# Late keys zeroed by GpSimd, a running maximum for 256 queries, and TensorE ordered by array mode, in a top-k attention and expert layer

## What is computed

```python
h = layernorm(x) * (1 + ca) + sa
q, k, v = (keep_largest(proj(h, w)) for w in (wq, wk, wv))   # one feature of 16 kept per head
scores = einsum('bhqd,bhkd->bhqk', q, k) / 4
scores = where(key later than query, -inf, scores)
scores = keep the 64 largest of each row, -inf elsewhere       # ties go to the earlier key
x = x + ga * (softmax(scores) @ v) @ wo.T
h = layernorm(x) * (1 + cb) + sb
x = x + gb * ffn(h)      # 8 experts, each takes the 512 tokens that want it most
```

## Time and profile before

| what | value |
|---|---|
| median of 3 runs (lowest, highest) | 1067.7 us (1066.64, 1073.47) |
| span of the profiled execution | 1065.8 us |
| attention, first to last score matmul | 65 to 720 us of the span |
| groups without other sequences' work | 32.8 us each |
| tile groups | 42.1 to 44.0 us |
| groups g = 0 that start and finish a sequence | 45.9 us |

### The profile page before, as it was taken

One profiled execution on the slowest core, in us unless ns is written; L12 is line 12 of the kernel. 1 busy time (PEld: TensorE's weight loads), 2 busy tenths in 40 slices (PEclk: granted clock), 3 DMA queues, 4 the chain that ended last, 5 costly groups with the idle time before them and its releaser, 6 DMA issues. The chain is left out here.

```text
span 1065.8 us, 17246 instructions
## 1 busy us (share of the span) xinstructions
PE 914.5 (86%) x6504; PEld 497.0 (47%) x6504; DVE 662.4 (62%) x1469; ACT 480.1 (45%) x631; POOL 268.7 (25%) x403
## 2 busy tenths in 40 slices
PE   6778999898999988999998999997204999999996
PEld 5533343444444443544445445335102666666664
DVE  6758677568587676676874775735487555543441
ACT  2635767664567745466773654661000122221110
POOL 3603222411331312122230220001003433343322
PEclk9869999999999998999998998998555999999999
DMA  4000000000100002100002011101561244442211
GB/s 145 15 1 21 1 21 1 1 1 2 61 21 1 1 2 81 60 1 2 1 1 81 2 41 44 38 1 40 198 221 37 51 114 107 112 115 41 25 20 20
DMA packets 34854, 46.57 MB, mean 44 GB/s; under 512 B 2184, under 2 KB 30928, under 8 KB 34640
## 3 DMA queue, kind: packets, MB, share of 16 engines
q1 hardware_dynamic: 28624, 36.89, 10.4%
q0 software_dynamic: 6144, 8.52, 5.0%
HBM read 32.69 MB, written 12.72 MB: 43 GB/s over the span
## 5 line engine op out<-in xcount | busy, mean ns | idle before, releaser
L947 ACT ACTIVATE p_buf<-ps 128x1024 f32<-128x1024 f32 x288 | 279.4, 1023 | 181.3 <-PE ps L424 95.6
L424 PE MATMUL ps<-qx,kd 32*128 32x512 f32 (+3 forms) x1280 | 147.0, 536 | 29.8 <-DVE p_buf L1281 26.1
L457 PE MATMUL ps<-p_buf,vv 128*17 128x512 f32 (+3 forms) x1664 | 156.1, 477 | 0.0
L2108 ACT ACTIVATE h_t<-ps,b_t 128x512 f32<-128x512 f32 x64 | 44.0, 688 | 236.7 <-PE ps L2048 236.7
L1281 DVE SCALAR_TENSOR_TENSOR p_buf<-ps,p_buf 128x1024 f32<-128x1024 f32 x64 | 76.7, 1220 | 78.0 <-ACT p_buf L947 65.0
L2048 PE MATMUL ps<-tok_t,w_sb 128*128 128x512 f32 x256 | 113.5, 602 | 0.0
L2058 PE MATMUL ps<-w_sb,h_t 128*128 128x256 f32 x512 | 112.5, 380 | 0.8 <-ACT h_t L2108 0.8
L779 POOL TENSOR_SCALAR_AFFINE_SELECT p_buf<-p_buf 128x512 f32<-128x512 f32 x64 | 42.0, 669 | 272.5 <-ACT p_buf L947 269.7
L2058 PEld LDWEIGHTS ps<-w_sb,h_t 128*128 128x128 f32 x512 | 96.6, 190 | 15.3 <-ACT h_t L2108 1.6
L424 PEld LDWEIGHTS ps<-qx,kd 32*128 32x128 f32 x1280 | 55.2, 191 | 71.6 <-issue 56.2
L365 PE MATMUL ps<-w_t,h_t 128*128 128x512 f32 (+1 forms) x224 | 78.8, 496 | 0.6 <-ACT w_t L889 0.6
(11 more groups left out here) (297 smaller groups left out, 1391.8 us busy)
## 6 DMA issues: line engine op xcount, KB each, us to landing
w_sb<-in_L_ffn_w_dram SPq DMA_DIRECT2D x16, 1024.0 KB, 8.8
h_table<-xr SPq DMA_DIRECT2D x3, 1056.0 KB, 4.6
x_in<-in_L_attn_x_dram SPq DMA_DIRECT2D x6, 512.0 KB, 3.9
out_dram<-xr SPq DMA_DIRECT2D x3, 1024.0 KB, 5.2
xr<-in_L_attn_x_dram SPq DMA_DIRECT2D x3, 1024.0 KB, 5.8
h_table<-xr SPq DMA_DIRECT2D x2, 528.0 KB, 3.0
xr<-in_L_attn_x_dram SPq DMA_DIRECT2D x2, 512.0 KB, 5.3
p_buf<-in_L_wmod_dram SPq DMA_DIRECT2D x1, 1024.0 KB, 8.6
```

The source lines that it names most:

```text
L424: m = pe.matmul(o, key, qx[r, par, t0:t0 + w], start=True, stop=not early)
L457: m = pe.matmul(ps[32 * h:32 * h + HD + 1, 6, o:o + w], vv[:, (gi // NG) % 2, i, HG * (gi % NG) + h, :], p_of(gi, u)[:, h, lo:lo + w], sta ...
L947: act.activation(p_of(gi, u)[:, 2 * a:2 * a + 2, :], buf(w), ACT.Exp, scale=0.25).then_inc(free_of(w)[0], 1)
L2108: act.activation(h1_t[:, f, :], ps[:, L1_BANKS[f % 3], :], ACT.Relu, bias=b1_t[:, e * FO + f:e * FO + f + 1]).then_inc(s_h1, 1)
```

## The change

1. `late` is gone. GpSimd's `tri` now also runs for units 0 and 1 and zeroes every diagonal block, eight a group where it was four. Values of units 0, 1, 2, 3 and 8 wait for it. In GpSimd's order `tri(gi, 0)` and `tri(gi, 1)` stand just ahead of `tri(gi, 2)`, behind `keep` of the first tile and `first_rstd`.
2. The running maximum and its correction cover 256 queries (`RUN`): `over` runs on 128 columns of unit 0 and 256 of unit 1, and `mx`, `qm`, their scan and the reduction beside it change length. The factor in `over` becomes -0.625.
3. TensorE's order in a block becomes scores and `chosen`'s first matmuls, then whole-array steps, then values. `chosen(gi, 0, 1)` moves behind unit 2's scores, `chosen(gi, 1, 0)` behind unit 5's, `chosen(gi, 1, 1)` behind unit 6's; `project` moves ahead of the values; unit 4's values go behind unit 5's, at the end of block 7; `lost` moves from the end of a group to behind unit 0's scores of the next.
4. VectorE follows: `negatives(gi)` at a group's start, `mask(gi, 1, 0)` ahead of `keys` (and behind the second norm and the layer norm's statistics), `mask(gi, 1, 1)` behind `keys` and behind `one_feature` of the third tile. ScalarE takes `out_bank(gi-1, 1)` after `evict_y`.

```diff
-        DIAG = (2, 3, 8)
+        DIAG = (0, 1, 2, 3, 8)
...
-                        early = t0 < 512
-                        diag = early and t0 == P * i
+                        run = max(min(RUN - t0, w), 0)
...
-                        for h in range(HG * diag):
-                            o = buf(("S", gi, u, h // 2))[:, h % 2, lo:lo + P]
-                            m = pe.matmul(o, identb[:, :], late[:, :], start=False, stop=True)
+                            o = buf(("S", gi, u, h // 2))[:, h % 2, lo:lo + run]
+                            m = pe.matmul(o, over[r, :], qm[r, par, t0:t0 + run], start=False, stop=True)
...
                 def pv(gi, u):
-                    if u in (3, 8):
+                    if u in DIAG:
                         pe.wait_ge(f_tri, tri_of(gi, u))
...
                     scores(gi, 0)
+                    lost(gi)
                     if gi:
                         pv(gi - 1, 7)
...
                     scores(gi, 1)
                     chosen(gi, 0, 0)
+                    if more:
+                        rows("K0", n)
+                    if tiles:
+                        project(b + 1, t0)
                     if gi:
                         pv(gi - 1, 8)
...
+                    scores(gi, 2)
                     chosen(gi, 0, 1)
                     if more:
                         rows("K1", n)
                     pv(gi, 0)
...
                     scores(gi, 5)
+                    chosen(gi, 1, 0)
...
                     scores(gi, 6)
+                    chosen(gi, 1, 1)
                     turn_back(gi, 0)
-                    pv(gi, 4)
...
                     if tiles:
                         keep(b + 1, t0)
+                    tri(gi, 0)
+                    tri(gi, 1)
                     tri(gi, 2)
                     tri(gi, 3)
...
+                    mask(gi, 1, 0)
                     if more:
                         keys(n)
                     if tiles:
                         one_feature(b + 1, t0 + 2)
+                    mask(gi, 1, 1)
                     out_rows_of(gi, 0)
```

## The result

The changed kernel takes 1111.3 us (1107.8 to 1113.5) against 1070.2 for the kernel before beside it: ratio 1.039, interval 1.035 to 1.043. The span of the profiled execution grew from 1065.8 to 1111.4 us, all of it in attention: from unit 1 of the first group to the end of attention it is 736.4 us after 689.0 (unit 1 begins 1.5 us earlier), and the experts' part takes 306 us in both. That is 45.6 us where the medians differ by 41.1: the profiled execution of the kernel before lies 2.5 us under that median, the one after 2.0 above its own.

A forecast was written before the change was run, and what follows sets the result against it. Attention was taken as bound by TensorE's own work and its waits: -30.6 work, -11.5 order, -41 waits that leave, +73 GpSimd wait with clock, +43 VectorE waits, sum +33 us. That gave 1067.7 + 33 = 1101 us, range 1070 to 1124.

The forecast's parts named there:

- Work that leaves: Units 0 to 2 on TensorE: `late` and shorter `over` save 1.91 us a group, 30.6 us in 16 groups.
- Order: TensorE's blocks: six fewer array mode changes a group on average, 0.12 us each, save 11.5 us.
- the rival of dear mode changes: TensorE's mode changes cost 0.29 us instead of 0.12, 38 us less: 1063 us, no change; chance 0.14.
- The new wait for GpSimd: Unit 0's values wait for `tri(gi, 0)` behind `keep` or `first_rstd` in nine groups, adding 60 us.
- Nothing is paid back: Behind the waits at unit 0's values ScalarE and VectorE run dry too, so the waiting is not recovered.
- Clock: TensorE's half-clock stretches, 1.4 us each: 13 us added behind nine GpSimd waits, 11 saved at unit 5's scores.
- the 6 us at `spread_mod`: Half clock behind `spread_mod`'s wait for VectorE in four groups finishing a sequence, 1.4 us each.
- Waits that leave and new ones for VectorE: Waits at unit 5's scores and `lost` leave, 41 us with clock; waits at `zero_rank`, `spread_mod` add 43 net.
- the ring: With second masks' entries behind units 5 and 6, unit 5's scores no longer wait for a mask: 25 us saved.
- GpSimd in time: Rival at unit 0's values: `tri(gi, 0)` done when TensorE arrives, 73 us go: 1028 us; chance 0.07.
- Masks at 1.70 us: Grown-waits rival: GpSimd's masks at 1.70 us in the nine-wait chain, +19 us; chance 0.17 for grown waits together.
- The half clock: Grown-waits rival: half clock twice as long behind the 13 long waits, +18 us; chance 0.17 for grown waits together.

The follow-up runs named there:

- Experiment 2: Kernel before with the work's part alone (`late` gone, eight masks, 256 queries), old orders, `tri(gi, 0)` and `tri(gi, 1)` first on GpSimd: 1043.9 us, ratio 0.977.
- experiment 7: Kernel before with the new order of `lost`, `chosen(gi, 0, 1)`, `rows`, `project` and `out_bank`, second masks' order excluded: 1071.2 us, ratio 1.001.
- experiment 5: Changed kernel with `tri(gi, 0)`, `tri(gi, 1)` and `tri(gi, 2)` moved to the head of GpSimd's group: 1051.7 us, ratio 0.983.
- experiment 3: Kernel before with the order's part of the change alone (points 3 and 4), `late` and `over` as before: 1087.8 us, ratio 1.015.
- Experiment 10: Experiment 2 with `tri(gi, 0)` and `tri(gi, 1)` behind `first_rstd` and `keep`, TensorE's order still old: 1094.2 us, ratio 1.023.
- experiment 12: Changed kernel with matmuls that nobody reads filling the nine waits ahead of unit 0's values: 1093.8 us, ratio 1.022.
- experiment 6: Kernel before with the second masks' new order alone, unit 4's values behind unit 5's with it: 1076.1 us, ratio 1.007.
- experiment 4: Changed kernel with `tri(gi, 0)`, `tri(gi, 1)` first on GpSimd, `chosen(gi, 1, 1)` behind `chosen(gi, 1, 0)`, both second masks ahead of `keys`: 1058.2 us, ratio 0.991.
- experiment 8: Experiment 2 with `tri(gi, 2)` first too, `chosen(gi, 1, 0)` behind unit 5's scores, `chosen(gi, 1, 1)` behind the small steps after: 1058.9 us, ratio 0.989.

## Why the prediction was right

It said 1101 us in 1070 to 1124, slower; 1111.3 came, and the forecast's own mechanism, the wait for GpSimd, made most of it. That the number came so near is partly luck, since errors of both signs cancel. In attention the profiled executions differ by 47.4 us where the sum has 33: the clock took some 10 us more than forecast and waits for ScalarE 16 more, while waits for VectorE took 8 less, and 2 to 3 us more of work left than forecast. By its steps:

- **Work that leaves, 30.6 us.** Experiment 2: 31.6 us of busy time. In the kernel before unit 0 goes from its scores (692.01) to the values behind it (694.18 in the earlier trace rows) in 2.17 us, in the kernel after from its scores to `lost` in 1.20: 0.97 us less, where 0.93 was forecast. One row of the kernel before, two of the kernel after:

```profile
692.01 0.93 PE L424 MATMUL ps<-qx,kd 32*128 32x384 f32 x8
...
483.55 0.93 PE L421 MATMUL ps<-qx,kd 32*128 32x384 f32 x8
...
484.75 0.23 PE L400 MATMUL ps<-upto,lw 128*128 128x128 bf16 x1
```

- **Order, 11.5 us.** Right in size, as far as runs tell: 13.0 us of busy time in experiment 7, 11.2 between experiments 2 and 5, and 4.9 in experiment 3, where the clock took some 8 us back (17 us more at 0.50). The bound of 0.29 us a change is out, and with it the rival of dear mode changes: by it experiment 2 would have lost 52 us of busy time, not 31.6. The Trainium skill (TensorEngine Tiling (Array Packing), Key Properties) has TensorE drain at each change; no run here shows more than the 0.12 us estimated from the earlier trace rows for one.
- **The new wait for GpSimd, 60 us.** 59.9 in nine waits; in a tile group 6.2 to 6.5 (6.4 forecast), in the two g = 0 5.5 (5.6), in the first 10.9 (10.6). The chain from the mask's start took 6.65 us of the 6.9. Experiment 10 gave 44.0 us where 44 was worked out in the same way. A chain of durations through in-order engines can be summed from the old trace.
- **"Nothing is paid back".** Nearly: wait (60) and clock (17.5) are 77 us, and three masks moved take 60 off. From the kernel after to experiment 5 idle time falls by 46 us only: 2.2 us of waiting for GpSimd stay, scores wait 7 us longer for ScalarE, and the waits for VectorE grow by 5.
- **Clock, 13 us behind the nine waits, 11 back at unit 5's scores.** Both missed to the same side. The nine waits cost 17.5 us by experiment 12. And nothing came back: in experiment 6 the wait at unit 5's scores is gone, and TensorE is busy at the granted clock 0.50 for 67 us of attention, after 65. With the 6 us at `spread_mod` the sum has 8 us for the clock; in the kernel after 105 us run at 0.50, 40 more than before, some 18 us lost (estimate by 2.09 against 1.14 us for a unit of scores).
- **Waits that leave and new ones for VectorE, -41 and +43.** The wait at unit 5's scores went, as said, and new ones came at `zero_rank`, `spread_mod` and scores of units 6 and 7. Without the clock the step makes these waits 8 us longer; they did not change: TensorE waits 46.0 us for VectorE in attention before, and 46.0 after. Up to the last score all fourteen kernels have 35 to 44 us of them. So TensorE's order chooses where it waits for VectorE, and hardly how long in all. That VectorE's chain of masks, `keys` and `out_rows_of` is what fixes this sum is argued, not shown; and VectorE doesn't set the pace alone, since experiment 2 took 31.6 us off TensorE's work and these waits stayed at 40 us up to the last score.
- **What the sum lacked: ScalarE.** Scores, transposes and projections wait 17.8 us for it in the kernel after (three lines shown), where scores waited 3.5 before; in all it is 23.6 us in attention after 7.1. The step that failed is the ring: I followed it for VectorE's masks alone. Single `chosen` entries between the units leave the next unit's scores with an entry that was given out later than before, and ScalarE has only just begun to read it. The places bear this out. Of the 10.7 us of scores, 9.4 stand at units 2, 3 and 7, each next in the ring behind a single `chosen`, where the kernel before has 0.3. Experiment 7, which parts only the first two, has the waits at units 2 and 3 and none at 7. Behind the fourth, at unit 6, it is only 0.4 us, so the account isn't complete.

The same two gaps show in experiment 3, expected at -10 and found at +18: ScalarE's waits and the clock, with no GpSimd wait worth naming (3.0 us).

The other rivals: GpSimd in time did not happen. Masks at 1.70 us did not carry the result, since the chain's masks ran at 0.64 us or less (five in 2.99 us), but for one of 1.70 in the first group. The half clock did last longer than forecast, 1.9 us a wait instead of 1.4, but not twice as long.

## What to carry to other kernels

Work given to an idle engine is only as early as what stands ahead of it in that engine's list: go through the list from the head, and through what each item waits for, before calling it hidden. Moving three calls on GpSimd was worth 60 us here, more than the 31 us of work that the change takes off TensorE. Moving a wait for VectorE along TensorE's list gained nothing here (experiments 3, 4, 6 and 8), and brought waits for ScalarE; taking work off TensorE did gain (experiment 2). Shortening VectorE's chain was not tried. Before moving an entry of a shared ring, follow it for every engine that reads it.

## What the runs showed of the hardware

These long waits of TensorE cost more than their length: the granted clock stood at 0.50 for 3.4 us behind a wait of 6.32, and filling nine waits with matmuls that nobody reads gave back 17.5 us. A shorter wait may or may not cost the clock. These two rows of the kernel after are the same scores (unit 6) of two groups, behind the same work and a wait of the same length; only the second ran at half speed:

```profile
410.33 1.14 PE L421 MATMUL ps<-qx,kd 32*128 32x512 f32 x8 [2.87 <-DVE p_buf L1269]
...
601.29 2.09 PE L421 MATMUL ps<-qx,kd 32*128 32x512 f32 x8 [2.87 <-DVE p_buf L1269]
```

GpSimd's mask is 0.64 us alone, and up to 2.71 beside VectorE's scan, more than the 1.70 of the earlier trace rows. Timeline of the kernel after:

```profile
507.23 2.29 DVE L1212 TENSOR_TENSOR_SCAN left<-k_not,minus 128x1024 bf16<-128x1024 bf16 x1
...
507.26 2.69 POOL L767 TENSOR_SCALAR_AFFINE_SELECT p_buf<-p_buf 128x512 f32<-128x512 f32 x1 [4.38 <-ACT p_buf L935]
```

The mask begins with the scan, which leaves off at 509.52, and ends 0.4 us behind it. The Trainium skill (SBUF — State Buffer, Terms) says that the two engines hold a shared pair of ports for a whole instruction and the other one blocks; this row agrees with it. All seven masks of 1.7 us and more in this kernel lie beside this scan. 78 of its 128 masks overlap no VectorE instruction, and the median stays at 0.64; 29 of those that do overlap one still take under 0.7 us.
